# An attention and expert kernel: router products by four pairs, score blocks by pairs, rank computation and first weights moved

## The reference

```python
xn = _layernorm(x)
# attention over the 4 heads of each token: scores are 4x4 per token
q = (xn @ Wq + bq).reshape(b, s, h, d); k, v alike with Wk, Wv
qr, qi = (q * cos(phase), q * sin(phase)); kr, ki = (k * cos(phase), k * sin(phase))
scores = (einsum('bshd,bsgd->bshg', qr, kr) + einsum('bshd,bsgd->bshg', qi, ki)) / sqrt(d)
s = (swap(einsum('bshg,bsgd->bshd', softmax(scores), v))) @ Wo + bo
# experts: router, Sinkhorn normalisation over 1024 tokens, the best 2 of 8
gates = _sinkhorn((einsum('btd,ed->bte', xn, router_w) + router_b) / max(temp, 0.1))
topk_vals, topk_idx = top_k(gates, 2); topk_gates = topk_vals / sum(topk_vals)
all_out = einsum(relu(xn @ wg[e]) * (xn @ wp[e]), wo[e])       # only the chosen two are used
g = silu(xn + sum(all_out[chosen] * topk_gates))
out = x + s * g
```

## Time and profile before

| | |
|---|---|
| median of 3 runs | 1550.58 us (1550.56 to 1554.21) |
| profiled execution | 1555.48 us, span in the trace 1553.7 us |
| PE busy | 1497.1 us, 96% of the span (PEld 1175.4, 76%) |
| DVE, ACT, POOL busy | 916.5 (59%), 788.9 (51%), 750.6 us (48%) |
| mean granted TensorE clock | 0.99 |

### The profile page before, as it was taken

One profiled execution on the slowest core, in us unless ns is written; L12 is line 12 of the kernel. 1 busy time (PEld: TensorE's weight loads), 2 busy tenths in 40 slices (PEclk: granted clock), 3 DMA queues, 4 the chain that ended last, 5 costly groups with the idle time before them and its releaser, 6 DMA issues.

```text
span 1553.7 us, 31511 instructions
## 1 busy us (share of the span) xinstructions
PE 1497.1 (96%) x11036; PEld 1175.4 (76%) x11036; DVE 916.5 (59%) x1730; ACT 788.9 (51%) x1269; POOL 750.6 (48%) x881
## 2 busy tenths in 40 slices
PE   5999799989999999999999999999999999999997
PEld 2546665758888888888888888788887878778775
DVE  7567889954444444444444444466765666576567
ACT  4767334413333333333333333566767776676674
POOL 4504188913666665444444444235365364734365
PEclk9999999989999999999999999999999999999999
DMA  9946432266474746242422351233576555556654
GB/s 324 392 162 216 173 137 72 75 215 228 158 247 158 242 156 241 75 165 77 157 76 89 133 213 56 92 135 123 189 244 218 181 188 179 187 193 202 218 178 136
DMA packets 181330, 267.93 MB, mean 172 GB/s; under 512 B 15944, under 2 KB 123264, under 8 KB 180800
## 3 DMA queue, kind: packets, MB, share of 16 engines
q1 hardware_dynamic: 149920, 196.79, 37.1%
q0 software_dynamic: 12960, 35.41, 6.9%
q10 hardware_dynamic: 18304, 33.72, 6.1%
HBM read 157.97 MB, written 107.89 MB: 171 GB/s over the span
## 4 chain that ended last, share of the span: by engine, by line
PE 83%; DVE 7%; ACT 4%; DMA 3%; issue 2%; SPq 1%; ACTq 0%; DVEq 0%
PE ps L1377 24%; PE ps L1300 18%; PE ps L1396 12%; PE ps L1319 8%; PE ps L1242 5%; PE ps L1386 4%; PE ps L1315 2%; PE ps L1359 2%; ACT WM L964 2%; PE ps L1191 2%; PE ps L1263 2%; PE ps L1119 1%; DMA u_d<-UN 1%; PE ps L1109 1%; DVE UN L1462 1%
## 5 line engine op out<-in xcount | busy, mean ns | idle before, releaser
L1377 PE MATMUL ps<-WR,FR 128*128 x1620 | 405.6, 400 | 1.9 <-DMA WR<-w_d 1.9
L1377 PEld LDWEIGHTS ps<-WR,FR 128*128 128x128 f32 x1620 | 296.2, 190 | 57.0 <-issue 2.1
L775 POOL DMA_INDIRECT y_d<-AUX x135 | 133.6, 990 | 297.0 <-DVE AUX L1943 295.5
L964 ACT ACTIVATE WM<-ps,bcs,trig 128x512 f32<-128x512 f32 x256 | 242.2, 1014 | 63.7 <-PE ps L1300 59.6
L1960 DVE TENSOR_TENSOR AUX<-AUX,ps 128x512 f32<-128x512 f32 x135 | 92.9, 688 | 304.7 <-ACT AUX L1011 304.7
L1011 ACT ACTIVATE AUX<-ps 128x512 f32<-128x512 f32 x135 | 80.6, 597 | 291.2 <-PE ps L1377 291.2
L1870 DVE TENSOR_SCALAR WM<-ps,vec,trig 128x512 f32<-128x512 f32 x208 | 196.6, 1031 | 46.8 <-ACT WM L964 46.6
L1300 PE MATMUL ps<-XH,WH 128*128 128x512 f32 x512 | 208.1, 407 | 7.8 <-issue 4.0
L1396 PE MATMUL ps<-WR,ABR 128*128 x540 | 207.1, 418 | 0.0
L1300 PE MATMUL ps<-XH,WL 128*128 128x512 f32 x512 | 200.6, 392 | 0.0
L1300 PE MATMUL ps<-XL,WH 128*128 128x512 f32 x512 | 200.6, 392 | 0.0
(11 more groups left out here) (268 smaller groups left out, 2497.7 us busy)
## 6 DMA issues: line engine op xcount, KB each, us to landing
US<-u_d SPq DMA_DIRECT2D x62, 512.0 KB, 4.7
u_d<-UN SPq DMA_DIRECT2D x120, 256.0 KB, 2.4
WR<-w_d SPq DMA_DIRECT2D x96, 256.0 KB
AUX<-y_d SPq DMA_DIRECT2D x32, 512.0 KB, 6.4
w_d<-WR ACTq DMA_DIRECT2D x24, 512.0 KB, 3.4
WM<-in_L_attn_x_dram SPq DMA_DIRECT2D x16, 512.0 KB, 9.6
xn_d<-WM SPq DMA_DIRECT2D x32, 256.0 KB, 6.2
mhl_d<-UNR ACTq DMA_DIRECT2D x16, 512.0 KB, 3.1
```

The lines of the kernel that those rows point to most:

```text
L775: e.indirect_dma_start(y_d, bass.IndirectOffsetOnAxis(toks[:, n:n + 1], 0), YS[n % 4], None).then_inc(s_y[n % 4], 16)
L964: e.activation(rotated(q, 2 * x, i), b, ACT.Identity, bias=bcs[:, x, 0, i:i + 1], scale=trig[:, 0, i:i + 1]).then_inc(s_ca, 1)
L1377: mm = e.matmul(b[:, :], x, WR[:, bass.ds(off[m] + (2048 * z + 1024 * a + 512 * k), 512)], start=(k == 0 and x is xh and z == 0), stop=(k ...
```

## The change

1. **Router part.** `rmm` takes four pairs together: for each half of the 256 values, four products into the four strips in turn (two per pair and eight per call, as before). RT gets six places (four more in RTX, which lies where XH and XL are used later). Of eight tiles VectorE normalises three (ON_DVE), ScalarE five.
2. **Rounds 0 to 3 by pairs.** Two score blocks share a bank, each in its own half, so four need no wait among themselves. `soft_a`, `soft_b` and `spread` are the pair versions throughout.
3. **k rotations.** In rounds 1 to 3 ScalarE does both rotations of pieces 8 to 15.
4. **Ranks.** `ranks` is cut in five parts after c = 8 to 12 of round 1, `slotted` follows c = 13 and 14, and the gates (`shares`) c = 15. Marks and placements start at (1, 24) and are denser: 16, 65 and 47 in rounds 1 to 3, where there were 25, 59 and 44.
5. **End of round 3.** `listed` stands on VectorE after c = 23 ahead of the last `mixed`, without `seli`; `xgl(0)` stands within the softmax steps. The results of round 3's mixes have four places of their own (ROX), so `mixed` doesn't wait for stores there; the first expert's `relu` does, and its product with it.
6. **First weights.** SP issues the twelve loads of expert 0 within round 3, from c = 4 of the u pieces on (`load_first`).
7. **Gates by DRAM.** `weigh` goes; SP writes the gates to DRAM in round 2 and reads them in the wanted order in round 3, four loads.

```diff
+        RTX = sb("RTX", [128, 4, 512])
+        XH, XL = XHL[:, 0:2, :], XHL[:, 2:4, :]
...
+        ROX = AUX[:, 1024:2048].rearrange("p (a d) -> p a d", d=D)
...
+        RT = [AB[:, 0, :], AB[:, 1, :], RTX[:, 0, :], RTX[:, 1, :], RTX[:, 2, :], RTX[:, 3, :]]
...
-            return q >= QE and c in (10, 11, 14, 15)
+            return 8 <= c < 16 if 0 < q < QE else c in (10, 11, 14, 15)
...
-            if (q, c) >= (1, 20):
-                pace += 1.5 if c < 16 else 2.4 if c < 24 else 4.0
+            if (q, c) >= (1, 24):
+                pace += 1.8 if c < 16 else 2.6 if c < 24 else 4.0
...
+        ON_DVE = (1, 3, 7)
+
+        def on_act(n):
+
+            return sum(i % 8 not in ON_DVE for i in range(n))
...
+            if 4 * QE - 8 <= n < 4 * QE - 4:
+                return ROX[:, n % 4, :]
...
+            def load_first(c):
+
+                e.wait_ge(s_ch, at(QE - 1, 16 + c))
+                for w in (512 * c, 4096 + 512 * c):
+                    if w < 6144:
+                        e.dma_start(WR[:, place_e(0) + w:place_e(0) + w + 512].bitcast(F32),
+                                    w_d[0:128, w:w + 512]).then_inc(s_wl, 16)
...
+                    if q == 2:
+                        e.wait_ge(s_gw, 1)
+                        e.dma_start(gate_d, gate.rearrange("p k n -> p (k n)")).then_inc(s_gd, 16)
+                    if q == 3:
+                        e.wait_ge(s_gd, 16)
+                        for h in range(H):
+                            e.dma_start(GP[h:128:4].rearrange("p i k q -> p i (k q)"),
+                                        gate_d.rearrange("(i r) (h f) -> h r i f", i=4, h=H)[h]).then_inc(s_gp, 16)
...
+                        if q == QE - 1 and c >= 4:
+                            for a in {4: (0, 1, 4), 5: (2, 3, 5)}.get(c, (c,)):
+                                load_first(a)
...
-            for i in range(4):
-                e.wait_ge(s_wst[i], 32 * len(range(i, NP, 4)))
-            e.wait_ge(s_hs[0], 16 * len(range(0, NH, 3)))
-            e.wait_ge(s_md, 16)
-            e.wait_ge(s_ch, 24 * QE)
-            load_expert(0)
...
-                if i >= 2:
-                    e.wait_ge(s_rm, i - 1)
-                e.activation(RT[:, i % 2, 0:512], (bT, bH)[i % 2][:, :], ACT.Copy).then_inc(s_rtc, 1)
+                if i >= 6:
+                    e.wait_ge(s_rm, 4 * ((i - 6) // 4 + 1))
+                e.activation(RT[i % 6], (bT, bH)[i % 2][:, :], ACT.Copy).then_inc(s_rtc, 1)
...
-                for n in (2 * i, 2 * i + 1)[:2 - i % 2]:
-                    e.activation(X[:, n, :], X[:, n, :], ACT.Identity, bias=nmr[:, n:n + 1],
-                                 scale=rstd[:, n:n + 1]).then_inc(s_xn, 1)
+                for n in (2 * i, 2 * i + 1):
+                    if n % 8 not in ON_DVE:
+                        e.activation(X[:, n, :], X[:, n, :], ACT.Identity, bias=nmr[:, n:n + 1],
+                                     scale=rstd[:, n:n + 1]).then_inc(s_xn, 1)
...
+                    for i in range(2):
+                        e.wait_ge(s_rs[i], 16 * 2 * (QE - 1))
...
-            def rmm(i):
-                e.wait_ge(s_rtc, i + 1)
-                g, a = i // 4, 32 * (i % 4)
-                if a == 0 and g >= 4:
+            def rmm(g):
+                e.wait_ge(s_rtc, 4 * g + 4)
+                if g >= 4:
                     e.wait_ge(s_re, g - 3)
                 for k in range(2):
-                    mm = e.matmul(ps[g % 4][a:a + 32, 0:256], rwT[:, k, :], RT[:, i % 2, 256 * k:256 * k + 256],
-                                  start=(k == 0), stop=(k == 1))
-                mm.then_inc(s_rm, 1)
+                    for a in range(4):
+                        mm = e.matmul(ps[g % 4][32 * a:32 * a + 32, 0:256], rwT[:, k, :],
+                                      RT[(4 * g + a) % 6][:, 256 * k:256 * k + 256], start=(k == 0), stop=(k == 1))
+                mm.then_inc(s_rm, 4)
...
-            for i in range(NT // 2 + 1):
-                if i < NT // 2:
-                    rt(i)
-                if i == 1:
+            for i in range(NT // 2):
+                rt(i)
+                if i == 5:
                     e.wait_ge(s_rwl, 2)
-                if i >= 1:
-                    rmm(i - 1)
+                if i >= 5 and i % 4 == 1:
+                    rmm(i // 4 - 1)
                 if i >= 10 and i % 4 == 2:
                     back(i // 4 - 2)
+            rmm(7)
...
-                if n >= 2:
-                    e.wait_ge(s_sm1, n - 1)
+                if n >= 4:
+                    e.wait_ge(s_sm1, n - n % 4)
+                to = 256 * (n % 2)
                 for c in range(4):
                     for x in range(2):
                         for h in range(2):
                             for a in range(2):
                                 row = 64 * a
                                 col = 128 * (4 * (n % 4) + c) + row
-                                mm = e.matmul(pS[n % 2][row:row + 64, 64 * c:64 * c + 64].rearrange("p (g t) -> p g t", g=H),
+                                mm = e.matmul(pS[n % 4 // 2][row:row + 64, to + 64 * c:to + 64 * c + 64].rearrange("p (g t) -> p g t", g=H),
...
-            def weigh():
...
-            weigh()
...
-                for n in range(a + 3, b, 4):
+                for n in (n for n in range(a, b) if n % 8 in ON_DVE):
...
+                gv = gate.rearrange("p k n -> p (k n)").rearrange("p (h k b z) -> p k b h z", h=H, k=2, b=NB)
+                for k, v in enumerate((v1, v2)):
+                    ins = e.tensor_tensor(gv[:, k], v.rearrange("p (b h z) -> p b h z", b=NB, h=H),
+                                          rec.rearrange("p (b h z) -> p b h z", b=NB, h=H), ALU.mult)
+                ins.then_inc(s_gw, 1)
...
+            def ranks(k):
...
-            side[24 + 3] = ranks
-            side[24 + 6] = lambda: slotted(0, oh1)
-            side[24 + 9] = lambda: slotted(1, oh2)
+            for k in range(5):
+                side[24 + 8 + k] = lambda k=k: ranks(k)
+            side[24 + 13] = lambda: slotted(0, oh1)
+            side[24 + 14] = lambda: slotted(1, oh2)
+            side[24 + 15] = shares
...
-                if 2 <= n < 4 * QE - 4:
+                if 2 <= n < 4 * QE - 8:
...
+                        if q == QE - 1 and c == 23:
+                            listed()
                         if 0 < q < QE:
-                            if c in (16, 18, 20, 22):
-                                spread(n + (c - 16) // 2)
-                                biased(n + (c - 16) // 2)
+                            if c == 16:
+                                spread(n)
+                                biased(n)
+                            elif c == 18:
+                                biased(n + 1)
+                            elif c == 22:
+                                biased(n + 3)
                             if c in mixes(q):
                                 mixed(n + mixes(q)[c])
+                            if c == 20:
+                                spread(n + 2)
+                                biased(n + 2)
...
-                        listed()
-                    for i in range(4):
-                        n = 4 * q + i
-                        soft_a(n)
-                        if i:
-                            soft_b(n - 1)
-                        if (q, 24 + i) in firsts:
-                            marks(firsts[q, 24 + i])
-                    soft_b(4 * q + 3)
-
-            segment(0, QE)
+                        xgl(0)
+                    soft_b(n)
+                    marks((*firsts.get((q, 26), ()), *firsts.get((q, 27), ())))
+                    soft_b(n + 2)
...
-            xgl(0)
-            e.wait_ge(s_gp, 1)
-            e.tensor_copy(GP[:, :, :, :].rearrange("p i k q -> p (i k q)"), pD[:, 0:128]).then_inc(s_gp, 1)
```

208 lines of the change are left out of this document (83 added, 125 removed).

## The result

The changed kernel takes 1531.17 us (median of 4, 1530.68 to 1533.93), the kernel before 1550.95 (median of 4): ratio 0.9855, 95% interval 0.9833 to 0.9877. The forecast was 1517, with 1510 to 1528 as its range: the direction was right, the time was 14 us too low. Two later executions of the kernel before, of 5224 and 2481 us, fell in a slower state of the chip and are left out throughout. The profiled execution of the changed kernel took 1531.26 us, its span is 1529.5.

A forecast was written before the change was run, and what follows sets the result against it. TensorE was taken as full from 357.1 us on, so gains lay before that: 8.5 + 7.2 + 6 + 11.5 = 33.2 us, from the 1550.58 median to 1517 us, range 1510 to 1528.

The forecast's parts named there:

- A: Router part ahead of round 0: products grouped over four strips overlap, ScalarE bounds next; gain 8.5 us, bounds 2 and 11.
- VectorE's extra tiles: Router part: two of ScalarE's last 26 instructions, 0.486 us each, move to VectorE; its six earlier extra normalisations add 2.7 us.
- B: End of round 0: four score blocks run at once without waiting for VectorE; gain 7.2 us, bounds 5 and 7.3.
- C: Rounds 1 to 3: ScalarE's k rotations and moved ranks remove TensorE's waits and clock loss; gain 6 us, bounds 2 and 7.5.
- the forecast's sign: Round 1: TensorE would show no wait over 1 us, with the clock at 1.00 there.
- T: Round 3's scores into the expert tiles: first up product 11.6 us after scores start; gain 11.5 us, bounds 8 and 12.5.
- Rival 3: Start of expert tiles: gathers land late behind weights and u loads; T = 6, total 1523 us; chance 0.09.
- The base: Starting time for the forecast: median of three, 1550.58 us, 4.9 below the profiled execution's 1555.48; gives 1517.4 instead of 1522.3.
- rival 1: Router part: strips don't overlap, TensorE keeps 1.57 us per pair; A is 2, total 1524 us; chance 0.10.
- rival 2: Rounds 0 to 3 give back what they gain: C = 0 and B = 5, total 1526 us; chance 0.13.
- rival 4: Rounds 1 to 3: ScalarE bounds the k pieces, total 1545 us; chance 0.03 within 0.3% (with mishaps), 0.03 slower.
- rival 5: Score blocks: an unnoticed wait keeps them apart; no size or chance of its own given.

The follow-up runs named there:

- b_again: The kernel before, with one register operation added per expert tile and a like one per expert on SP: median 1553.91 us (10 runs).
- a_again: The changed kernel, with one register operation added per expert tile and a like one per expert on SP: median 1530.55 us (4 runs).
- dve4: The changed kernel, but VectorE normalises two tiles of eight and ScalarE six, as before in number: median 1529.97 us.
- score_wait: The changed kernel, but the third and fourth score blocks of rounds 0 to 3 wait until VectorE has read the first pair's bank: 1537.48 us.
- k_dve: The changed kernel, but VectorE makes the sin rotations of the k pieces of rounds 1 to 3 again: median 1540.22 us.
- ranks3: The changed kernel, but ranks and slotted stand at their old places in round 1, with ScalarE's k rotations kept: median 1532.24 us.
- gt_order: The changed kernel, but first gathered rows are copied and split ahead of the last pair's softmax, register loads ahead of the last score block: median 1528.68 us.
- go_stores: The changed kernel with first rows copied and split before the last softmax, register loads before the last score block, and round 3's last two result stores earlier: 1524.15 us.
- late_w: The changed kernel, but the twelve loads of the first weights stand after round 3's transfers, as before: 1537.93 us.

## Why the prediction was wrong

**A**, 8.5 forecast, 7.1 measured (8.1 from b_again to a_again): right in its mechanism and its next bound. The 128 router products take 11.2 us in all instead of 35.7, as forecast (10 to 13), though three of their eight groups ran at a granted clock of 0.5 to 0.9. Against rows 3, ScalarE's last copy ends at 66.82 instead of 74.46:

```profile
66.22 0.60 ACT L876 ACTIVATE AB<-ps 128x512 f32<-128x512 f32 x1 [0.25 <-PE ps L1133]
```

Its last stretch, from the first normalisation behind the last statistics (53.77), takes 13.05 us instead of 17.25, where I had 12.2, and starts 3.4 us earlier, where I had 3.8. The term that failed in it is VectorE's extra tiles: dve4 gives VectorE two of eight again, ScalarE's stretch then has 26 instructions instead of 24 and takes 13.19 us, 0.14 more and not 1, and the part ends 0.3 us earlier, which is within what it varies (67.2 to 69.3).

**B**, 7.2 forecast, 8.3 measured in the first pair of traces and 6.3 in the second; score_wait gives back 8.0 of the first: right.

**C**, 6 forecast, 4.8 measured (3.9 in the second pair): right in its mechanism (k_dve, ranks3). What the waits at the scores of rounds 1 and 2 gave, new small waits took: TensorE waits 1.67 us once for a bias addition in round 1, where the forecast's sign was no wait over 1 us.

**T**, 11.5 forecast, 6.7 measured: here the working failed, in three terms of its sum and in one thing that it left at nothing. The path to the first up product was 14.35 us, not 11.6: 1.5 for the pause in the scores, and 1.3 for the second tile's transposes and the register loads, which are in the order of the kernel and which I hadn't counted. The low clock cost 2.2, where I had some 0.6. These make 4.3 of the 4.8 us that are missing; the other 0.5 is within scatter. And "the stores of the results, which only the first expert's relu waits for" had been costed at nothing. In the first trace of the changed kernel they land at 321.69, a microsecond ahead of that relu (322.75), and cost nothing yet; in a_again the relu waits for them. Had the path come out as forecast, they would have taken the gain: with the start at 11.4 T is 661.2 (gt_order), and with the stores moved as well 657.0 (go_stores), 10.4 us less than before. Rival 3 was right that the gathers come later behind the weights, and wrong that it decides; that its number for T, 6, is nearer than mine is chance.

**The base.** I took 4.9 us off because the profiled execution stood that far above a median of three. Ten runs of the kernel before (b_again) have a median of 1553.91: the execution lay 1.6 us above that, and the median of three 3.3 below, so most of what I took off was the scatter of three runs. Taken from that execution's own time, the forecast is 1522.3 against 1531.26, which is 9.0 short: 4.8 of T, 1.4 of A, 1.2 of C, less 1.1 of B, and 2.7 of chance in the last stage.

Of the rivals, none came: strips do overlap (rival 1), rounds 1 to 3 kept 4.8 us and B all (rival 2), ScalarE's k pieces hold up nothing (rival 4), and what parts the score blocks of round 3 isn't a wait that went unnoticed in the order (rival 5) but goes with the early weights (late_w).
